# Centering context tiles on the scalar engine, and scaling the queries straight out of PSUM

## The reference, cut to what matters

```
xn = layernorm(ctx, ln_x_g, ln_x_b)          # (x - mean) / sqrt(var + 1e-5) * g + b, per row of 256
ln = layernorm(layernorm(x), ln_l_g, ln_l_b)
q = ln @ Wq
k, v = [xn; ln] @ Wkv                        # 1024 + 64 keys per batch
qn = rmsnorm(q per head, qn_g) * 64**-0.5    # q / sqrt(mean(q*q)) * gain
kn = rmsnorm(k per head, kn_g)
out = softmax(qn kn^T) v
x = x + out @ Wout + bout
x = x + self_attention(layernorm(x)) ; x = x + ffn(layernorm(x))
```

## Time and profile before

| | us |
|---|---|
| median of 3 runs | 239.11 (238.82 to 239.4) |
| the profiled execution | 238.49 |
| its span, first to last instruction | 236.7 |
| PE busy | 224.9 (95%) |
| DVE busy | 153.8 (65%) |
| ACT busy | 149.7 (63%) |
| POOL busy | 80.7 (34%) |

### The profile page before, as it was taken

How to read it: one execution, slowest core, us unless ns; L and a number is a source line. 1 busy time by engine, 2 the same in 40 slices (tenths; PEclk the granted TensorE clock), 3 DMA queues, 4 the chain that set the end, 5 groups by cost and what they waited for, 6 DMA issues and landing times.

```text
span 236.7 us, 4203 instructions
## 1 busy us (share of the span) xinstructions
PE 224.9 (95%) x1475; PEld 194.5 (82%) x1475; DVE 153.8 (65%) x346; ACT 149.7 (63%) x329; POOL 80.7 (34%) x127
## 2 busy tenths in 40 slices
PE   7588999999999999999999999999999998999994
PEld 6364887886788989888898989899999987999883
DVE  1779999998887876967767655566675530312541
ACT  4255589888886869686766567778777655015141
POOL 5368876773473647464250500000000010100200
PEclk9799999999999999999999999999999999999999
DMA  6875101100000000000000799600000000000000
GB/s 176 303 214 216 47 24 28 42 25 22 0 25 0 0 6 0 0 0 3 0 0 3 264 424 322 151 3 0 0 4 0 0 4 0 0 3 0 0 3 22
DMA packets 11236, 13.80 MB, mean 58 GB/s; under 512 B 1584, under 2 KB 9936, under 8 KB 10960
## 3 DMA queue, kind: packets, MB, share of 16 engines
q1 hardware_dynamic: 10944, 13.01, 16.9%
q10 hardware_dynamic: 272, 0.52, 0.6%
HBM read 13.14 MB, written 0.13 MB: 56 GB/s over the span
## 4 chain that ended last, share of the span: by engine, by line
PE 71%; DVE 13%; ACT 4%; issue 3%; DMA 3%; POOL 2%; SPq 1%; ACTq 0%; DVEq 0%; POOLq 0%
PE banks L1158 19%; PE banks L1025 14%; PE banks L1072 9%; PE banks L1101 8%; PE banks L1287 5%; DVE small L784 4%; PE banks L1179 4%; DMA rows<-in_L_xattn_ln_x_b 3%; PE banks L1172 3%; DVE sk L796 3%; PE banks L1103 2%; PE banks L1210 2%; PE banks L1312 1%; DVE raw L752 1%; DVE small L791 1%
## 5 line engine op out<-in xcount | busy, mean ns | idle before, releaser
L819 DVE TENSOR_TENSOR ptl<-banks,pth 128x512 fp32r<-128x512 f32 (+1 forms) x48 | 26.8, 558 | 26.2 <-ACT pth L578 25.3
L1158 PE MATMUL banks<-xnh,pth 128*128 128x256 f32 x128 | 37.6, 294 | 0.0
L1158 PE MATMUL banks<-xnh,ptl 128*128 128x256 f32 x128 | 36.3, 283 | 0.0
L1158 PE MATMUL banks<-xnl,pth 128*128 128x256 f32 x128 | 36.2, 283 | 0.0
L578 ACT ACTIVATE pth<-banks 128x512 fp32r<-128x512 f32 (+1 forms) x48 | 23.7, 494 | 10.3 <-PE banks L1025 9.2
L461 POOL TENSOR_TENSOR small<-small 128x16 f32<-128x16 f32 x7 | 20.4, 2908 | 27.3 <-DVE small L791 27.3
L525 ACT ACTIVATE sk<-banks 128x512 f32<-128x512 f32 x36 | 20.6, 606 | 14.2 <-PE banks L1072 14.1
L796 DVE TENSOR_TENSOR sk<-banks,small 128x512 f32<-128x512 f32 x36 | 23.0, 679 | 6.9 <-POOL small L461 6.9
L784 DVE TENSOR_REDUCE small<-sk 128x8 f32<-128x512 f32 x36 | 23.6, 679 | 5.3 <-ACT sk L525 5.1
L442 POOL COPY sp<-sp 128x64 f32<-128x64 f32 x16 | 4.1, 254 | 62.8 <-ACT sp L559 62.8
L1158 PEld LDWEIGHTS banks<-xnh,pth 128*128 128x128 f32 x128 | 24.5, 192 | 0.4 <-issue 0.4
(11 more groups left out here) (177 smaller groups left out, 480.9 us busy)
## 6 DMA issues: line engine op xcount, KB each, us to landing
knT<-in_L_attn_qkv_kernel SPq DMA_DIRECT2D x1, 3072.0 KB, 12.1
raw<-in_ctx SPq DMA_DIRECT2D x16, 128.0 KB, 2.1
knT<-in_L_xattn_Wq SPq DMA_DIRECT2D x1, 1024.0 KB, 9.2
wv<-in_L_xattn_Wkv SPq DMA_DIRECT2D x1, 1024.0 KB, 5.1
wout_sb<-in_L_xattn_Wout SPq DMA_DIRECT2D x1, 1024.0 KB, 5.5
knT<-in_L_attn_out_kernel SPq DMA_DIRECT2D x1, 1024.0 KB, 15.6
wraw<-in_L_xattn_Wkv ACTq DMA_DIRECT2D x1, 512.0 KB, 4.2
wraw<-in_L_xattn_Wkv SPq DMA_DIRECT2D x1, 512.0 KB, 6.1
```

Source lines behind the costliest of these rows:

```text
L819: nc.vector.tensor_tensor(ptl[:, j0:j1, :], banks[:, t3_bank(u, c), 0:(j1 - j0) * P].rearrange("p (j r) -> p j r", j=j1 - j0), pth[:, j0:j ...
L1158: nc.tensor.matmul(banks[:, u_bank(u), 0:D], p_[:, j, :], x_, start=(j == 0 and i == 0), stop=False)
```

## The change

Centering of tiles 1 to 11 (`FA + 3` is 11) moves from DVE to ACT: an ACTIVATE computes `scale * in + bias` with scale = rstd and bias = -mean * rstd. POOL makes that bias column (`nmr`) with one more instruction, linked behind the power instruction. On ACT the centering of tile 1 stands behind `xt_high(1)`, that of tile 2 behind `context_high(1)`, and that of tile `i + 2` behind the square root of item `i`, ahead of `xt_high`. The queries no longer pass through `qT`: `keys_out` of the query item writes them scaled from PSUM to the block diagonal, four instructions of 64 partitions instead of two of 128, and the four copies at items 5 to 8 and their semaphore go. The mask piece of item 4 is moved to item 6, the latents' high half from item 3 to item 7.

```diff
+        def centered_by_act(k):
+            return 1 <= k <= FA + 3
+        nmr = small[:, 212:216]
...
             def tile_rstd(k):
                 pool.wait_ge(mv_ready, k + 1)
-                rsqrt_var(mv[:, k % 4, :], ve[:, k % 4:k % 4 + 1], rstd[:, k % 4:k % 4 + 1], 1e-5).then_inc(rstd_ready, 1)
+                last = rsqrt_var(mv[:, k % 4, :], ve[:, k % 4:k % 4 + 1], rstd[:, k % 4:k % 4 + 1], 1e-5)
+                if centered_by_act(k):
+                    link(last)
+                    last = nc.gpsimd.tensor_scalar(nmr[:, k % 4:k % 4 + 1], mv[:, k % 4, 0:1], -1.0, rstd[:, k % 4:k % 4 + 1],
+                                                   ALU.mult, ALU.mult)
+                last.then_inc(rstd_ready, 1)
...
+            def tile_center(k):
+                act.wait_ge(rstd_ready, k + 1)
+                nc.scalar.activation(raw[:, k % 4, :], raw[:, k % 4, :], ACT.Identity, bias=nmr[:, k % 4:k % 4 + 1],
+                                     scale=rstd[:, k % 4:k % 4 + 1]).then_inc(xhat_ready, 1)
...
                 if i == QI:
-                    ins = nc.scalar.activation(qT[:, h, :], bank, ACT.Copy)
+                    act.wait_ge(qg_ready, 1)
+                    act.wait_ge(zeroed, 1)
+                    pairs = qbd[:, :, :].rearrange("p (b g) i -> p b g i", b=B)
+                    for e in range(2):
+                        e0, e1 = e * DH, (e + 1) * DH
+                        ins = nc.scalar.activation(pairs[e0:e1, :, 4 * h:4 * h + 4, e * M:(e + 1) * M],
+                                                   bank[e0:e1, :].rearrange("p (g b i) -> p b g i", g=4, b=B), ACT.Copy,
+                                                   scale=qg[e0:e1, 3:4])
...
             xt_high(1)
+            tile_center(1)
             squares(0, 1)
...
-                    if 5 <= i < 9:
-                        queries(*divmod(i - 5, 2))
                     context_high(i)
+                if i == 1:
+                    tile_center(2)
                 act.wait_ge(n2_ready, i + 1)
                 nc.scalar.activation(sd[:, i % 2, :], n2[:, i % 2, :], ACT.Sqrt).then_inc(sd_ready, 1)
+                if i > 0:
+                    tile_center(i + 2)
                 if i + 2 != QI and i + 2 <= ITEMS_A:
                     xt_high(tile(i + 2))
-                if i in (4, 9):
+                if i in (6, 9):
                     act.wait_ge(w_mask, 32)
                     mask_bias(0, i == 9)
-                if i == 3:
+                if i == 7:
                     act.wait_ge(w_lat, 16 * 2 * B)
                     nc.scalar.activation(lnhl[:, :, :], lat2, ACT.Copy).then_inc(lnh_ready, 1)
...
             xt_low(1)
-            tile_center(1)
             key_norm2(0, 1)
...
                 if i == 0:
                     tile_stats(2)
-                else:
-                    tile_center(i + 2)
...
                 if i == 0:
-                    tile_center(2)
                     tile_stats(3)
                     tile_sums(4)
```

More of the change, by code:

```diff
@@ L109, in perceiver_layer @@
         lat2 = early(0, 0, B * D).rearrange("p (b d) -> p b d", b=B)
-        qT = early(1, 0, INNER).rearrange("p (h n) -> p h n", h=2)
         lnTf = early(3, 0, D).rearrange("p (c r) -> p c r", c=DC)
@@ L216, in perceiver_layer @@
         qg_ready = sem("qg_ready")
-        qbd_ready = sem("qbd_ready")
         s_ps = sem("s_ps")
@@ L544, in keys_out @@
                 ins.then_inc(kt_ready, 1)
[L546 to L555, removed]
             def exponentials(u):
@@ L565, in unit_high @@
                 act.wait_ge(kt_ready, 2 * (ITEMS_A if b == 0 else ITEMS))
-                act.wait_ge(qbd_ready, 4)
                 if u == 1:
@@ L1085, in logits @@
                 if u == 0:
-                    pe.wait_ge(qbd_ready, 4)
                     pe.wait_ge(kt_ready, 2 * ITEMS_A - (1 if part == 1 else 2))
```

## The result

The changed kernel takes 245.16 us (median of 4 runs, 244.62 to 245.72) against 238.98 for the one before: ratio 1.0256, with a 95% interval of 1.0224 to 1.0288. Slower by 6.2 us, where the sum had 4.8. The time lies 1.3 us above the forecast of 243.9 and just inside the stated range (240.8 to 245.2). One execution of experiment 8 and one of the kernel before, both in a slower state (321 and 769 us), are left out of all times.

The account below looks back on a forecast made before the run. PE and DVE were full in the first half's tiles; the lengthened ACT/DVE loop would move the last reciprocal from 58.05 to 62.84, +4.8 us: 238.49 becomes 243.3, and the median's 0.6 gives 243.9, range 240.8 to 245.2.

Parts of the forecast that it names:

- the sum: Delays added up through the first half's items: last reciprocal at 62.84 against 58.05, +4.8 us.
- Centering leaves DVE: On DVE between clamp and reciprocal: the 0.41 us centering lies in a wait that stays; only 1.8 us excess could return.
- Centering enters ACT's loop: Behind ACT's square root: 0.51 us per item, lengthening ACT's loop from 3.49 to 4.00, past PE's 3.85.
- The collision: DVE's clamp waits for POOL's low half in plain items: 4.34 us instead of 4.00; upper end 0.4.
- The bias column: One more POOL instruction per tile, 0.27 us each, eleven times; exposed in the head, where tile 3's centering starts at 22.15.
- The queries: Item 4 on ACT: four scaled copies of 0.59 us, 2.36 in all, replace two of 0.95 together: +1.41.
- Signs that I gave: In the later profile: ACT idle under 0.5 us before plain square roots, item 4's near 35.9, last reciprocal near 62.8.
- rival D: Centerings and queries fit ACT's waits; DVE's 1.8 us excess returns, 1.0 in the full stretch: 237.3 us, chance 0.08.
- B: First half bound by ACT without the clamp meeting POOL's low half, plain items 4.00: +3.1, 242.2 us, chance 0.26.
- C: Cheap ends: centering 0.31, queries 0.48 each, no collision, PE's 3.85 rules: +1.2, 240.3 us, chance 0.14.
- E: POOL's bias column costs 0.55, so the loop with the collision is 4.62: +6.8, 245.9 us, chance 0.04.

Follow-up runs that it names:

- experiment 8: Kernel before with POOL's bias column for tiles 1 to 11 added but read by nobody, DVE still centering: 240.26 us, ratio 1.0062.
- experiment 3: Changed kernel without POOL's low halves of context tiles 2 to 9, which are zeroed once at the start: 242.63 us, ratio 1.0153.
- experiment 4: Changed kernel with ACT's centering of tiles 4 to 11 moved ahead of the same item's square root: 241.62 us, ratio 1.0103.
- experiment 9: Changed kernel with tiles 1 to 3 centered by DVE again, without their bias columns: 244.64 us, ratio 1.0243.
- experiment 7: Changed kernel with centering of tiles 4 to 11 ahead of the square root, queries as before, no clamp in items 0 to 10: 238.95 us, ratio 0.9994.
- experiment 6: Kernel before without the clamp in items 0 to 10, division in the square root's scale, floor left out: 236.28 us, ratio 0.9884.

## Why the prediction was right, and where it was not

The direction and the mechanism came true: a longer loop through ACT and DVE, lengthened again by a collision with POOL. The size was 1.3 us short. The measured 245.16 is above the 243.0 to 244.9 that the text gives this mechanism, and it lies inside the whole range by 0.04 us, which is luck. Which terms were too small or left out is told below.

*Centering leaves DVE: nothing comes back.* Right. The reciprocal waits 0.28 us for the square root in all nine items from which the centering was taken; DVE's time from the start of the clamp to the reciprocal did not shrink (0.83 in item 3, 30.49 to 31.32, with a long clamp; 0.46 before).

*Centering enters ACT's loop.* Right: 0.49 from start to start (0.51 taken), and 3.99 for a plain item with the collision gone (experiment 3) against 4.00. That place and not amount decides is shown by experiment 4, 3.5 us for the same instructions elsewhere. (The copy that the prediction has 0.12 behind the square root is that of the transposed tile, L508, not the context copy.) The Trainium skill (ScalarE: Activation LUTs, What ACT_TABLE_LOAD costs) had given 0.585 and 0.49; the trace has a mean of 0.587 over eight and 0.49, so here the rule was better than my own sum from rows.

*The collision.* Right in mechanism and size: plain items of 4.36 against 4.34, 2.5 us by experiment 3 (2.3 expected). That the item agrees so closely is in part two errors that cancel: the column put 0.32 between the power instruction's end and the low half, not 0.27, and the centering was 0.58 long, not 0.62. I did not count it in item 2, where the clamp took 0.54: a term left out, 0.37 us. That its upper end is 0.4 was wrong: 0.60 of excess (0.77) in experiment 4; a low half of 0.74 against a clamp of 0.17 would have said so. The Trainium skill (SBUF — State Buffer, Who interferes with whom) has the port pair that DVE and GpSimd share held for a whole instruction; the traces agree, down to the clamp that starts together with an instruction of POOL and waits for the whole of it.

*The bias column.* The term was mis-sized. It moves the next instruction of POOL by 0.37 (21.50 to 22.39 is 0.89, against 0.52 before), not 0.27: between the end of the power instruction (22.05) and the start of the column (22.16) pass another 0.11 us. Two columns make 0.2 of it. ACT and the square root of item 2 (start, us):

```profile
22.46 0.60 ACT L521 ACTIVATE raw<-raw,small 128x256 f32<-128x256 f32 x1 [1.04 <-POOL small L429]
...
26.71 0.22 ACT L640 ACTIVATE small<-small 128x16 f32<-128x16 f32 x1 [1.12 <-DVE small L803]
```

22.46 for 22.15, and with the uncounted collision 26.71 for 26.03: 0.68 of the 1.47 us by which the last reciprocal (64.31) missed its forecast (62.84). The other 0.1 of the head goes with its start: the square root of item 0 comes at 16.74, where it was 16.55, behind squares that start at 15.10 and not at 14.63, right behind the centering of tile 1, which I had said would not move the path. Two executions alone cannot tell this from their scatter (17.31 in experiment 9, with the head of the kernel before). Alone, the column costs 1.5 us (experiment 8); the prediction had no number for that.

*The queries.* Mis-sized: 2.79 for the four and not 2.36, 0.43 us, and above the upper bound of 0.61 each that I gave. Out of PSUM with a scale column they are 0.68 long and 0.70 from start to start, so nothing overlaps; I had subtracted 0.11 for each. A further 0.13 went into item 4's clamp.

*A term that wasn't there.* PE waited twice for the query copies, ahead of its key transposes:

```profile
33.46 0.63 PE L1033 MATMUL banks<-ident,sk 128*128 128x128 f32 x4 [1.06 <-ACT qbd L552]
...
34.86 1.09 PE L1033 MATMUL banks<-ident,sk 128*128 128x128 f32 x4 [0.77 <-ACT qbd L552]
```

After that its granted clock was lower: 0.51 of full speed from 35.0 to 38.3, which is the level of 1.2 GHz, and 1.00 from 38.3 on. The projection of item 5 came late and ACT's second square of that item waited for it until 39.85: item 5 took 4.50 for 4.34. This need not come with the edit. In the profile of experiment 9, with the same copies and waits of PE of 1.03 and 0.77 us, the clock stayed at 1.00 and item 5 took 4.36; experiments 3 and 4 (waits of 0.69 and 0.55, then 0.77) show no lower clock there either. So the waits alone do not bring the lower clock, and what does is not shown.

The rest of the items agree to 0.04 us: among them 4.73, 4.63, 4.36 and 4.57 (the last to the reciprocal) against 4.72, 4.63, 4.34 and 4.59.

*Signs that I gave.* The square root of item 4 came at 37.14 and not near 35.9, the last reciprocal at 64.31 and not near 62.8, by the terms above. One sign was wrong in kind: ACT's idle time ahead of the square root did not vanish in plain items, it is 1.13 us. A loop through two engines leaves each of them idle while the other works, so an engine in the bounding loop need not look busy. I had named this idle time as the room for the edit (rival D) and, in the same text, its end as the sign of the opposite.

*Rivals.* B (no collision) had 242.2, and the kernel of experiment 3, where POOL is out of the way, took 242.6; it has the same too small terms for head and queries as my sum. C fails by the centering of 0.59 and the queries of 0.68. E's 245.9 lies nearer to the 245.16 than my 243.9, but not for its reason: it had 0.55 for the column, where 0.37 was measured. D held that 1.8 us of long centerings could come back, 1.0 in the full stretch. In experiment 7 room was made on ACT, and nothing came back over the kernel before, though by experiment 6 the kernel with PE as its bound is 2.8 us faster and not 1.8.

## What to carry to other kernels

Before work is moved to an engine with idle time, follow the loop of waits once round and write down its length: an instruction put behind a wait in that loop costs its full length from start to start each time round (0.49 us here), and the same ones put into the idle time ahead of the wait cost 3.5 us less in all (experiment 4). An instruction taken off a full engine gives nothing if it stood in the shadow of a round trip. Here the same trace showed the thing worth removing, a tiny clamp on the round trip between two engines: without it the kernel before is 1.2% faster, and 0.9% faster with its floor kept as a bias.

## What the runs showed that I had not expected

- A clamp of 0.17 us on DVE took 0.77 where it started together with an instruction of POOL (experiment 4): more than the 0.4 that I had taken as the worst case.
- One more 128x1 instruction per tile on POOL, 0.26 long, cost the whole kernel 1.5 us over eleven tiles (experiment 8). The prediction had put its price as low as nothing, with POOL idle; before the experiment I expected 1.1.
- In the changed kernel's profile, waits of PE of 1.06 and 0.77 us were followed by 3.3 us at the lower clock (0.51); in experiment 9's, waits of 1.03 and 0.77 us were not. One trace was not enough to tie a lower clock to the edit.
